# Cross-attention and ternary feed-forward on one core: ring piece 3 is loaded and summed behind the blocks of Wk

## The chip, the cores and the metric

The kernel runs on one core of a Trainium2 chip. The metric is the device time of one execution in microseconds, the median of several runs. The profile is one execution, taken by the hardware profiler; its span runs from the first to the last instruction.

## What is computed

```python
x   = layernorm(x)                                    # 16 x 256 x 512, fp32
q   = (ln(x) * g1 + b1) @ Wq + bq                     # 512 -> 512
k   = (ln(ctx) * g2 + b2) @ Wk + bk                   # 384 -> 512
v   = (ln(ctx) * g2 + b2) @ Wv + bv
x   = x_in + softmax(q @ k.T * 512**-0.5) @ v @ Wo + bo
h   = bitlinear(ln(x), w_fc) + gate * (ln(x) @ v.T @ fast_b.T @ u.T)   # 512 -> 2048
out = x_mid + bitlinear(relu(h) ** 2, w_proj)         # 2048 -> 512

def bitlinear(x, w):                                  # one scale for each row of w
    scale = max(mean(abs(w), axis=1), 1e-5)
    return x @ (clip(round(w / scale), -1, 1) * scale).T
```

The two weights of the feed-forward part are thus made ternary on the chip, which needs the sum of absolute values of each row first.

## The kernel before

The 4096 tokens are worked on in 8 groups of 512 tokens. For each group the attention part of the next group and the feed-forward part (16 `up` and 16 `down` blocks) of the current one are interleaved. Nearly all of the time goes there, and it is the same code before and after the change.

Ahead of the groups stands a setup, the prologue. It folds the attention weights, and makes the ternary weights. What matters here:

- `Wq` comes in four blocks, `Wk` in three, each of 256 KB. TensorE transposes them (`wqT:c`, `wkT:c`, L1185) into the banks H0 and H1 in turn; the product `bq` (L1190) lies between them. The results are read out by ScalarE or VectorE: `WqT` (L714, L902), the bq product into `x2a` (L910), `WkT` with the gains g2 multiplied in (L906).
- `M:c` (L1197) is the product of `WqT` and `WkT` for one block c of four. It is read twice: ScalarE makes its rounded half (L721), then VectorE, which waits for ScalarE, the rest (L913). `wvT:c` transposes Wv's blocks. A job n may use its bank only when job n-2 has been read: `wkT:1` waits for bq's evacuation, and `wvT:0` for `M:0` as read by VectorE.
- The feed-forward weights come in 32 pieces of 256 KB through a ring of 8 buffers (`ring:k`, L518), in groups of four. For each piece one engine sums absolute values: ScalarE (L846) most of them, VectorE (L1134) `abs:3`, `abs:7`, `abs:11` and a few more. When all four sums of a group are there, GpSimd makes the scales (`scale:j`, L670), VectorE their reciprocals (`invert:j`, L1122) and rounds the pieces (`round:k`, L1130). TensorE turns each (`turn:k`, L1378) and ScalarE stores its sign (`store:k`, L869). From piece 8 on a load waits until the buffer's piece has been rounded.
- `tb` makes the bias of the scores. GpSimd multiplies the three blocks of Wk by the evacuated bq product (L661, three instructions, each waiting for its Wk block); ScalarE sums each result (L836), one wait for each. Behind that ScalarE issues the load of Wo into the buffer that the products used (L840).
- Statistics: VectorE takes those of x (`xs01`, `xs23`, L1082 to L1091), GpSimd the power of them (`xs23`, L649, L650), ScalarE normalises (`nx0` and so on, L797), TensorE transposes the result (`n1T:t`, L1248).

The order of each engine is written out by hand in `PROLOGUE`. Each engine works its list strictly in order and waits on semaphores. The starts of the lists, of before:

```
pe    wqT:0 wqT:1 vecs wqT:2 wqT:3 bq:0 wkT:0 wkT:1 wkT:2 M:0 M:1 turn:0 turn:1 wvT:0 turn:2 turn:3 n1T:0 wvT:1 M:2
act   wqT:0 vecs wqT:2 abs:0 abs:1 wqT:3 g2 abs:2 tb Wo abs:4 abs:5 M:0 abs:6 M:1 nx0 wvT:0 store:0 store:1
dve   wqT:1 bqacc abs:3 bq:0 wkT:0 wkT:1 invert:0 wkT:2 xs01 xs23 abs:7 round:0 round:1 M:0 round:2 round:3
pool  scale:0 tb xs23 scale:1 scale:2 cs23
```

Of the kernel before, what the change touches and what calls it, by code (L numbers as in the profile page):

```python
# [199 lines left out]
def moved_by_act(b, kind):  # L200
# [3 lines left out]

PROLOGUE = {
# [4 lines left out]
    ).split(),  # L210
# [17 lines left out]
    ).split(),  # L228
    "dve": (
# [1214 lines left out]
```

## Time and profile before

| | |
|---|---|
| median of 3 runs | 780.21 us (779.91 to 780.46) |
| the profiled execution | 779.99 us, its span 778.2 us |
| TensorE busy | 766.5 us (98%) |
| VectorE busy | 547.6 us (70%) |
| ScalarE busy | 368.6 us (47%) |
| GpSimd busy | 107.4 us (14%) |

Times in the profile are microseconds from the start of the span. L12 is line 12 of the kernel. PE is TensorE, PEld its weight loads, DVE VectorE, ACT ScalarE, POOL GpSimd, SPq the sync engine's queue that issues DMAs. In a timeline a row begins with the start and the time that it covers; neighbouring instructions of the same kind are merged into one row (x8 is eight of them), and square brackets give the idle time before it and who ended it.

### The profile page before, as it was taken

How to read it: one execution, taken by the hardware profiler on the slowest of the kernel's cores; microseconds unless marked ns; L12 is line 12 of the kernel's file. 1: busy time of each engine (PE TensorE's matmuls, PEld its weight loads, DVE VectorE, ACT ScalarE, POOL GpSimd, SP SyncE). 2: the span in 40 equal slices, each digit the busy share in tenths (PEclk: the TensorE clock that was granted, in tenths of full speed). 3: DMA queues.
4: the chain of work that ended last, by engine and by line, in shares of the span. 5: the costliest groups of instructions: out<-in, count | busy, mean ns of one | idle time of the engine just before them, and what ended most of it. 6: DMA issues, size and time to landing. Idle time of an engine off the chain costs nothing.

```text
span 778.2 us, 10596 instructions
## 1 busy us (share of the span) xinstructions
PE 766.5 (98%) x3767; PEld 637.6 (82%) x3767; DVE 547.6 (70%) x1118; ACT 368.6 (47%) x690; POOL 107.4 (14%) x125
## 2 busy tenths in 40 slices
PE   7999999999999999999999999999999999999997
PEld 4678788888888888888888888888888888888886
DVE  5999766778676777667766786768667686656434
ACT  5998744354434535354434545254542644233332
POOL 3101300100211030110312020210202002100001
PEclk9999999999999999999999999999999999999999
DMA  8743431163115322063214422063212430040101
GB/s 315 248 150 109 63 88 41 21 96 87 56 40 84 58 72 85 13 97 69 81 42 65 65 75 96 1 99 70 90 41 41 75 88 1 1 54 9 47 0 55
DMA packets 180125, 56.20 MB, mean 72 GB/s; under 512 B 167620, under 2 KB 167894, under 8 KB 180072
## 3 DMA queue, kind: packets, MB, share of 16 engines
q1 hardware_dynamic: 149940, 50.79, 26.8%
q10 hardware_dynamic: 30132, 4.73, 3.8%
q8 instruction: 30, 0.49, 0.3%
q14 instruction: 23, 0.19, 0.1%
HBM read 26.92 MB, written 8.39 MB: 45 GB/s over the span
## 4 chain that ended last, share of the span: by engine, by line
PE 97%; DVE 1%; ACT 1%; issue 0%; DMA 0%; DVEq 0%; ACTq 0%
PE H L1357 30%; PE O L1338 29%; PE G L1220 26%; PE H L1363 4%; PE H L1220 1%; PE H L1197 1%; PE H L1204 1%; PE O L1412 1%; PE G L1304 1%; PE O L1378 1%; PE H L1185 1%; PE G L1248 0%; DMA Wq_s<-in_L_xattn_Wq_dram 0%; DVE x2a L1057 0%; PE O L1395 0%
## 5 line engine op out<-in xcount | busy, mean ns | idle before, releaser
L1338 PE MATMUL O<-projT,qbuf 128*128 128x512 f32 x992 | 242.1, 390 | 0.0
L1338 PEld LDWEIGHTS O<-projT,qbuf 128*128 128x128 f32 x992 | 185.0, 188 | 38.2
L779 ACT ACTIVATE rbuf<-H,scf 128x512 f32<-128x512 f32 x128 | 87.5, 684 | 124.9 <-DVE qbuf L1116 75.7
L1357 PE MATMUL H<-even_group,fcT 128*128 128x512 f32 x512 | 127.5, 391 | 0.0
L1357 PE MATMUL H<-odd_group,fcT 128*128 128x512 f32 x512 | 127.3, 391 | 0.0
L1112 DVE TENSOR_TENSOR rbuf<-rbuf 128x512 f32<-128x512 f32 x128 | 91.5, 723 | 45.9 <-ACT rbuf L779 45.9
L787 ACT ACTIVATE qbuf<-rbuf 128x512 fp32r<-128x512 f32 x125 | 78.5, 628 | 89.7 <-PE O L1338 62.7
L1116 DVE TENSOR_TENSOR qbuf<-rbuf,qbuf 128x512 fp32r<-128x512 f32 x125 | 85.9, 688 | 36.5 <-ACT qbuf L787 35.8
L1357 PEld LDWEIGHTS H<-odd_group,fcT 128*128 128x128 f32 x512 | 95.3, 188 | 19.3
L1357 PEld LDWEIGHTS H<-even_group,fcT 128*128 128x128 f32 x512 | 95.1, 188 | 19.2
L1220 PE MATMUL G<-Wvo,tT 128*128 128x512 f32 x270 | 64.7, 389 | 0.0
L1220 PEld LDWEIGHTS G<-Wvo,tT 128*128 128x128 f32 x270 | 50.6, 188 | 10.6
L1363 PE MATMUL H<-tstack,uT 128*128 128x512 f32 x128 | 49.8, 389 | 0.0
L654 POOL TENSOR_TENSOR nrs<-nrs,mhalf 128x1 f32<-128x1 f32 x32 | 25.5, 798 | 125.7 <-DVE nrs L954 125.7
L691 POOL TENSOR_TENSOR x2b<-xb,crow 128x512 f32<-128x512 f32 x16 | 24.3, 1550 | 120.2 <-DMA out_dram<-x2b 115.4
L741 ACT ACTIVATE pbuf<-G,nmax 128x256 f32<-128x256 f32 x29 | 13.7, 473 | 53.6 <-DVE nmax L941 53.6
L1220 PEld LDWEIGHTS G<-n2T,tT 128*128 128x128 f32 x261 | 34.1, 191 | 1.6
L1220 PE MATMUL G<-n2T,tT 128*128 128x256 f32 x261 | 34.8, 283 | 0.0
L760 ACT ACTIVATE tT<-G,tbias 128x512 fp32r<-128x512 f32 x23 | 15.8, 686 | 37.6 <-PE G L1220 37.6
L1220 PE MATMUL G<-odd_group,M 128*128 128x512 f32 x144 | 33.3, 389 | 0.0
L691 POOL TENSOR_TENSOR x2a<-xb,crow 128x512 f32<-128x512 f32 x12 | 17.5, 1489 | 112.6 <-DMA out_dram<-x2a 112.6
L1220 PEld LDWEIGHTS G<-odd_group,M 128*128 128x128 f32 x144 | 27.0, 188 | 5.6
(194 smaller groups left out, 989.0 us busy)
## 6 DMA issues: line engine op xcount, KB each, us to landing
xb<-in_x_dram SPq DMA_DIRECT2D x8, 1024.0 KB, 5.1
n_blocks<-n_rows SPq DMA_DIRECT2D x112, 64.0 KB, 2.3
ctxb<-in_ctx_dram SPq DMA_DIRECT2D x8, 768.0 KB, 4.3
n_blocks<-ctxb SPq DMA_DIRECT2D x112, 48.0 KB, 2.2
wring<-in_L_ffn_w_fc_dram SPq DMA_DIRECT2D x16, 256.0 KB, 6.2
wring<-in_L_ffn_w_proj_dram SPq DMA_DIRECT2D x16, 256.0 KB, 2.7
out_dram<-x2a SPq DMA_DIRECT2D x8, 512.0 KB, 2.7
x_blocks<-x_rows SPq DMA_DIRECT2D x56, 64.0 KB, 3.5
```

Source lines behind the costliest of these rows:

```text
L654: nc.gpsimd.tensor_tensor(nrs[:, t:t + 1], nrs[:, t:t + 1], mhalf[:, 0:1], ALU.pow).then_inc(rstd_made, 1)
L691: nc.gpsimd.tensor_tensor(x2[par][:, t, :], xb[:, t, :], crow[:, :], ALU.add).then_inc(res_made, 1)
L741: nc.scalar.activation(pbuf[:, t, :], bank[:, 0:S], ACT.Exp, bias=nmax[:, t:t + 1], scale=SM, accum_out=rowsum[:, t:t + 1]).then_inc(unit_ ...
L760: nc.scalar.activation(tT[:, HI, t, :], bank[:, :], ACT.Identity, bias=tbias[:, t:t + 1]).then_inc(unit_act, 1)
L779: nc.scalar.activation(rbuf[:, j % 2, :], banks[f"H{j % 2}"][:, :], ACT.Relu, scale=scf[:, j:j + 1]).then_inc(relu_made, 1)
L787: nc.scalar.activation(squares(b, j)[:, HI, :], rbuf[:, j % 2, :], ACT.Copy).then_inc(sqhi_made, 1)
L1112: nc.vector.tensor_tensor(rbuf[:, j % 2, :], rbuf[:, j % 2, :], rbuf[:, j % 2, :], ALU.mult).then_inc(square_made, 1)
L1116: nc.vector.tensor_tensor(squares(b, j)[:, LO, :], rbuf[:, j % 2, :], squares(b, j)[:, HI, :], ALU.subtract).then_inc(sqlo_made, 1)
L1220: mm = pe.matmul(bank, w, m, start=(first and i == 0), stop=(last and i == len(pairs) - 1))
L1338: mm = pe.matmul(banks[f"O{t}"][:, :], qbuf[:, j % 2, h, t * P:(t + 1) * P], projT[:, j, :], start=(j == 0 and h == HI), stop=(j == NFF - ...
L1357: pe.matmul(banks[f"H{j % 2}"][:, :], fcT[:, k, j * P:(j + 1) * P], xnT[:, h, k, :], start=(k == 0 and h == HI), stop=False)
L1363: pe.matmul(banks[f"H{j % 2}"][:, :], uT[:, j * P:(j + 1) * P], tstack[:, :], start=False, stop=True).then_inc(up_full, 1)
```

## The change

The order of loads on the SP queue was `Wk:2 ring:3 Wk:0 Wk:1 x:0`; it becomes `Wk:2 Wk:0 Wk:1 ring:3 x:0`. In VectorE's order the sum of ring piece 3 moves from before the evacuation of bq to behind those of Wk, and the reciprocal of the first group's scales from between the evacuations of Wk to behind the statistics of x. The lists of TensorE, ScalarE and GpSimd are the same.

```diff
@@ -204,7 +204,7 @@
 PROLOGUE = {
     "sp": (
-        "Wq:0 Wq:1 ring:0 Wq:2 bqrow ring:1 bo Wq:3 ring:2 Wk:2 ring:3 Wk:0 Wk:1 x:0 ring:4 ring:5 ring:6 "
+        "Wq:0 Wq:1 ring:0 Wq:2 bqrow ring:1 bo Wq:3 ring:2 Wk:2 Wk:0 Wk:1 ring:3 x:0 ring:4 ring:5 ring:6 "
@@ -227,7 +227,7 @@
     "dve": (
-        "wqT:1 bqacc abs:3 bq:0 wkT:0 wkT:1 invert:0 wkT:2 xs01 xs23 abs:7 round:0 round:1 M:0 round:2 round:3 "
+        "wqT:1 bqacc bq:0 wkT:0 wkT:1 wkT:2 abs:3 xs01 xs23 invert:0 abs:7 round:0 round:1 M:0 round:2 round:3 "
```

## Rows read from the trace of the kernel before

**Rows 1.** The page's first part: busy time, share of the span, instructions.

```profile
PE 766.5 (98%) x3767; PEld 637.6 (82%) x3767; DVE 547.6 (70%) x1118; ACT 368.6 (47%) x690; POOL 107.4 (14%) x125
```

**Rows 2.** Stretches: length; PE, PEld, DVE, ACT, POOL busy; granted clock; DMA.

```profile
20.00:23.00 3.00, 2.87 (x27) 2.42 (x25) 3.00 (x8) 3.00 (x6) 0.34 (x1) 1.00 0.96 341
23.00:40.00 17.00, 16.88 (x88) 9.67 (x86) 15.97 (x37) 16.57 (x38) 1.70 (x4) 1.00 0.73 225
40.00:60.00 20.00, 19.38 (x124) 15.53 (x125) 18.64 (x42) 18.11 (x45) 2.14 (x9) 1.00 0.48 154
60.00:100.00 40.00, 38.48 (x240) 32.75 (x241) 35.12 (x86) 30.45 (x63) 12.19 (x15) 1.00 0.35 78
```

**Rows 3.** The chain that ended last, 9 to 24 us: start, length, what.

```profile
13.48 0.17 DVE inverse_scales L1122
...
14.37 5.40 PE H L1197 x16
19.77 0.45 PE O L1378 x8
```

**Rows 4.** Timeline of TensorE, 3 to 22 us.

```profile
3.72 1.94 PE L1185 MATMUL H<-ident,Wq_s 128*128 128x128 f32 x8 [3.72 <-DMA Wq_s<-in_L_xattn_Wq_dram]
...
11.23 0.60 PE L1185 MATMUL H<-ident,Wk_s 128*128 128x128 f32 x4
...
20.05 0.61 PE L1185 MATMUL H<-ident,Wv_s 128*128 128x128 f32 x4
...
21.23 0.63 PE L1248 MATMUL G<-ident,nrm 128*128 128x128 f32 x4
```

**Rows 5.** Timeline of VectorE, 10 to 31 us.

```profile
10.26 0.69 DVE L1134 TENSOR_REDUCE asum<-wring 128x1 f32<-128x512 f32 x1 [0.85 <-DMA wring<-in_L_ffn_w_fc_dram]
11.43 0.69 DVE L910 COPY x2a<-H 128x512 f32<-128x512 f32 x1 [0.48 <-PE H L1190]
...
13.56 0.66 DVE L906 TENSOR_TENSOR WkT<-H,g2row 128x512 f32<-128x512 f32 x1
14.20 2.47 DVE L1082 BATCH_NORM_STATS2 xst<-xb 128x6 f32<-128x512 f32 x4
...
17.87 0.88 DVE L1130 TENSOR_SCALAR rounded<-wring,inverse_scales 128x512 f16<-128x512 f32 x2
19.23 0.62 DVE L913 SCALAR_TENSOR_TENSOR M<-H,vcols,M 128x384 fp32r<-128x384 f32 x1 [0.49 <-ACT M L721]
...
30.25 1.35 DVE L1134 TENSOR_REDUCE asum<-wring 128x1 f32<-128x512 f32 x2
```

**Rows 6.** Timeline of ScalarE, 15 to 21 us.

```profile
15.97 0.72 ACT L836 ACTIVATE x2a<-x2a,vcols 128x512 f32<-128x512 f32 x1 [0.42 <-POOL x2a L661]
...
18.57 0.56 ACT L721 ACTIVATE M<-H,vcols 128x384 fp32r<-128x384 f32 x1
...
19.80 0.58 ACT L721 ACTIVATE M<-H,vcols 128x384 fp32r<-128x384 f32 x1
```

**Rows 7.** Timeline of GpSimd, 11 to 33 us.

```profile
11.88 0.24 POOL L670 TENSOR_SCALAR scf<-asum 128x4 f32<-128x4 f32 x1 [9.07 <-ACT sprow L846]
12.21 3.73 POOL L661 TENSOR_TENSOR x2a<-Wk_s,x2a 128x512 f32<-128x512 f32 x3
17.45 1.34 POOL L649 TENSOR_TENSOR xrs<-xrs,mhalf 128x4 f32<-128x4 f32 x1 [1.51 <-DVE xrs L1091]
...
19.83 0.51 POOL L670 TENSOR_SCALAR scf<-asum 128x4 f32<-128x4 f32 x1 [0.77 <-ACT sprow L846]
31.08 0.23 POOL L670 TENSOR_SCALAR scf<-asum 128x4 f32<-128x4 f32 x1 [10.74 <-DVE asum L1134]
31.39 1.04 POOL L649 TENSOR_TENSOR crs<-crs,mhalf 128x4 f32<-128x4 f32 x1
```

**Rows 8.** Timeline of the SP queue: ring 3, then the two Wk blocks.

```profile
5.04 0.43 SPq L518 DMA_DIRECT2D wring<-in_L_ffn_w_fc_dram  x1
5.52 0.91 SPq L554 DMA_DIRECT2D Wk_s<-in_L_xattn_Wk_dram  x2
```

## The prediction

> **What bounds the kernel now.** The page's first part comes first: TensorE is busy 766.5 of 778.2 us [rows 1], so only what delays TensorE, or takes work from it, can move the time. The change lies wholly in the setup, so the stretches come next. TensorE is busy 2.87 of the 3 us from 20 to 23, 16.88 of 17 from 23 to 40, 19.38 of 20 up to 60 and 38.48 of 40 up to 100 [rows 2]. All its idle time from 20 to 100 us is 0.13 + 0.12 + 0.62 + 1.52 = 2.4 us: a delay put in at 20 us has nearly nothing behind it to vanish into. ScalarE is as full there (3.00 of 3.00, 16.57 of 17) and VectorE nearly so.
>
> Then the chain of waits through the touched place [rows 3, 5]: VectorE empties the bank of the bq product (11.43), the Wk evacuations follow with a 0.17 us reciprocal (`invert:0`) before the last of them (13.48), and TensorE computes M:0 and M:1 from 14.37 to 19.77. What it may do next is `turn:0 turn:1 wvT:0`; wvT:0 reuses M:0's bank and waits until VectorE has read it.
>
> The chain does not show what stands just beside it, so the engines' own orders are read. wvT:0 starts at 20.05 [rows 4]. VectorE's M:0 (19.23, 0.62 us, to 19.85) waited 0.49 us for ScalarE's M:0 [rows 5]. ScalarE did that at 18.57, directly behind `tb` (its third piece starts at 15.97), the issue of Wo, abs:4 and abs:5 [rows 6]. ScalarE's `tb` waits for GpSimd's three products, 12.21 to 15.94, and GpSimd runs them behind `scale:0`, at 11.88 [rows 7]. So a second chain, GpSimd's products, ScalarE's tb, M:0, reaches wvT:0 with a slack of about 0.1 us.
>
> **Part by part.** *The loads.* Ring 3 is issued at 5.04 [rows 8], between Wk:2 and Wk:0. Behind the change Wk:0 and Wk:1 go one place (0.48 us, the step from 5.04 to the next issue at 5.52) earlier and ring 3 two places (0.95) later. The SP queue issues the same number, and no wait stands between them; x:0 behind them keeps its place. Worth of the earlier Wk: nothing. wkT:0 starts at 11.23 directly behind the bq product [rows 4], and wkT:1 needs the bank that VectorE empties from 11.43 [rows 5]. Bounds: 0 to -0.2 us; I take 0. Ring 3 lands at about 10.26 now (VectorE starts its sum then, having waited on that transfer) [rows 5]; 1 us later is far ahead of its new use at 14.1.
>
> *VectorE.* abs:3 (0.69 us) leaves the place before bq:0. It ended at 10.95 and VectorE then idled 0.48 us for TensorE before 11.43 [rows 5], so its removal frees nothing. `invert:0` leaves the place before wkT:2: that evacuation starts at 13.48 in place of 13.56 [rows 3, 5], and M:0 and M:1 each 0.08 us sooner. This is the whole gain on TensorE, and it is worth something only if wvT:0 doesn't wait for the second chain. Behind wkT:2 abs:3 now runs from about 14.12 to 14.81. xs01, xs23, abs:7, round:0 and round:1 slide by 0.69 - 0.08, a little less for overlap: the statistics start at 14.73 in place of 14.20, round:0 at 18.48 in place of 17.87 [rows 5]. turn:0 could start at 19.69 and finds its piece at 18.96: hidden. VectorE still reaches its M:0 at about 19.35.
>
> *The wait that moves, which decides.* `scale:0` on GpSimd needs all four sums of group 0, abs:3 among them; GpSimd's order `scale:0 tb xs23` is not changed. So `tb` now stands behind a sum that VectorE does 3.86 us later. Step by step: abs:3 ends at 14.81. From such a sum to GpSimd's start is 0.15 us: the pair at 30.25 takes 1.35, its first half ends at 30.93 and scale:2 starts at 31.08 [rows 5, 7]. scale:0 runs 14.96 to 15.20 (0.24); the next GpSimd work starts 0.08 behind (31.08 + 0.23 to 31.39), hence 15.28. Before it was 12.21: later by 3.07 us. Products until 19.01 (3.73), ScalarE's third tb piece at 15.97 + 3.07 = 19.04, Wo's issue and abs:4, abs:5 behind, ScalarE's M:0 at 21.64, VectorE's at 22.30 to 22.92, wvT:0 at 23.06. TensorE, done with turn:1 at about 20.1, stands still for almost 3 us.
>
> Queued behind ScalarE's wait are the Wo load, abs:4 to abs:6, M:1 and nx0; behind VectorE's M:0 the rounds 2 onwards, and so the SP queue's ring loads 10 onwards and the loads behind them. The xs23 power on GpSimd (17.45 now) starts at 19.1 and ends by 20.6, ahead of nx0: hidden by the larger delay.
>
> *What is given back.* M:1 on ScalarE starts at 19.80, just after TensorE finished it at 19.77, though ScalarE's step before it allowed 19.65 [rows 3, 6]. With TensorE early, these 0.15 us come back: nx0 is late by 3.07 - 0.15 = 2.92, and n1T:0, which started at 21.23 for nx0's sake [rows 4], by the same. From there on TensorE, ScalarE and VectorE stand at the same points of their orders as before, and all DMAs gated by rounding move along. I find no wait on a load that is independent of them. Sum: +2.9 us.
>
> *Unknown sizes.* The third product (17.75 to 19.01) now lies beside round:0. Where GpSimd's work lies beside a round now, the power of 17.45 takes 1.34 against 1.04 us for that of 31.39, and scale:1 at 19.83 takes 0.51 against 0.23 [rows 7]. So the products may take 0 to 0.45 us more (the end is one round's 0.44, half the pair at 17.87 [rows 5]); I take 0, because the product starts first, and keep 0.45 for the range. The latency of 0.15 may be 0.05 to 0.2. Own range of the forecast: +2.6 to +3.5.
>
> The Trainium skill ("SBUF — State Buffer", "Who interferes with whom") says that VectorE in its two-port modes and GpSimd hold a shared port for a whole instruction, and the first to start makes the other wait. The two longer rows agree in direction. By it round:0 would wait for the third product, not the reverse, which leaves the sum as it is.
>
> **Rivals.** *(A) The clock falls too.* TensorE would have a hole of 2.9 us and then until 25 us only short transposes with waits between. The granted clock reads 1.00 in every stretch, but eight transposes take 1.94 us at the start (0.24 each) and four take 0.60 at 11.23 (0.15) [rows 2, 4]: the level of half speed (1.2 GHz) shows at the start, after TensorE had stood still, the full one (2.4 GHz) after it had worked. If it returns, 1.5 to 3.2 us of the work from 22 us on are paid twice: the upper end is half of the 6.3 us from 3.72 until the fast level was reached about 10, the lower half of that. Time 779.99 + 2.9 + 1.5 to 3.2 = 784.4 to 786.1. Against it: 40 us with 1.52 us of holes show no fall; no hole in this trace is near 3 us. Chance 0.13.
>
> The Trainium skill ("TensorE: Matmul & The Clock Gate", "HAM oscillation — how this bites in real kernels") states that idle gaps between bursts throttle the engine again. No row here has such a gap; by that rule the time is rival A's.
>
> *(B) The hole is closed again: not slower.* Place: the waits from 23 to 100 us. TensorE idles 2.26 us there [rows 2]; if these waits were bound to something that does not move (loads in flight), they would absorb that much of the 2.9 and leave 0.6 or so: 780.6. It decides from 1.4 us absorbed. Against it: those waits name VectorE and ScalarE, which stand behind the same late step, and the loads are gated by rounds. Chance 0.09, the half-absorbed cases among it.
>
> *(C) The second chain doesn't bite: the change does what it looks like.* M:0 0.08 us earlier and Wk up to 0.2: 779.7 to 779.9. It needs GpSimd's tb to start before abs:3; the code forbids it. Chance 0.03.
>
> **How the numbers follow.** Profiled execution of before: 779.99 (span 778.2 and 1.8 around it), 0.2 below the median 780.21. 779.99 + 2.9 = 782.9, on the median 783.1; I say 783.1, chance 0.75. Its own range is 782.6 to 783.9. The range reaches down to 782.0 for a part absorbed, and up to 785.2 into rival A: 782.0 to 785.2. A measurement can tell about 0.2%, 1.6 us, from no change. Slower: forecast, rival A and part of B, 0.90; within: 0.07; faster: 0.03 (what B and C leave for an effect not seen).
>
> **What would show it.** After the change: abs:3 at about 14.1, scale:0 near 15.0, products from 15.3, ScalarE's M:0 at 21.6, wvT:0 at 23.1, n1T:0 at 24.2, and the same distance of about 2.9 us in the steady part. The prediction is wrong if GpSimd's products start near 12.2, if TensorE has no hole after 20.1, if four transposes behind the hole take near 1 us (rival A), or if the offset shrinks between 25 and 100 us (rival B).

## The result and the profile after

The changed kernel takes 786.02 us (median of 5 runs, 785.73 to 789.66) against 780.21 us (779.85 to 780.46): 5.8 us more. The ratio over all runs is 1.0083 with a 95% interval of 1.0061 to 1.0106; it lies above the 1.0074 of the two medians because it takes in the run of 789.66. Forecast were 783.1 us, 2.9 us more, and a range up to 785.2. The sign and the first step were right; the size was half of what came.

TensorE's timeline of the changed kernel, 14 to 36 us; it answers to [rows 4]:

```profile
14.86 5.40 PE L1197 MATMUL H<-WkT,WqT 128*128 128x384 f32 x16 [0.89 <-DVE WkT L906]
20.09 0.61 PE L1378 MATMUL O<-identh,rounded 128*128 128x128 f16 x8
23.52 1.11 PE L1185 MATMUL H<-ident,Wv_s 128*128 128x128 f32 x4 [2.82 <-DVE M L913]
24.42 1.06 PE L1378 MATMUL O<-identh,rounded 128*128 128x128 f16 x8
25.28 1.06 PE L1248 MATMUL G<-ident,nrm 128*128 128x128 f32 x4
26.13 0.89 PE L1185 MATMUL H<-ident,Wv_s 128*128 128x128 f32 x4
26.86 2.75 PE L1197 MATMUL H<-WkT,WqT 128*128 128x384 f32 x8
...
30.55 0.60 PE L1248 MATMUL G<-ident,nrm 128*128 128x128 f32 x4
32.27 3.70 PE L1204 MATMUL H<-x2a,WvT 128*128 128x512 f32 x8 [1.11 <-DVE M L913]
```

Beside the same points of before (M:0 14.37, wvT:0 20.05, M:2 22.13, n1T:1 25.82, wvo:0 26.27) the lag grows in four steps: 0.49 us at M:0, 3.47 at wvT:0, 4.73 at M:2 and n1T:1, 6.00 at wvo:0. Behind that it stays: the span is 784.2 against 778.2, again 6.0. There are two holes, not one. The first (2.82 us) is the predicted one. Behind it four transposes (wvT:0, n1T:0) take 1.11 and 1.06 us instead of 0.61 and 0.63: the clock fell. The second (1.11 us, before wvo:0) no step of the prediction has.

GpSimd, 15 to 24 us, for [rows 7]: scale:0 now waits for VectorE's sum, and the products behind it take 3.73 us as before.

```profile
15.50 0.24 POOL L670 TENSOR_SCALAR scf<-asum 128x4 f32<-128x4 f32 x1 [12.69 <-DVE asum L1134]
15.82 3.73 POOL L661 TENSOR_TENSOR x2a<-Wk_s,x2a 128x512 f32<-128x512 f32 x3
```

VectorE, 14 to 33 us, for [rows 5]:

```profile
14.63 0.68 DVE L1134 TENSOR_REDUCE asum<-wring 128x1 f32<-128x512 f32 x1
...
18.99 1.24 DVE L1130 TENSOR_SCALAR rounded<-wring,inverse_scales 128x512 f16<-128x512 f32 x2
22.84 0.62 DVE L913 SCALAR_TENSOR_TENSOR M<-H,vcols,M 128x384 fp32r<-128x384 f32 x1 [2.61 <-ACT M L721]
...
28.57 0.75 DVE L1068 SCALAR_TENSOR_TENSOR bvrep<-x2a,vcols,borow 128x512 f32<-128x512 f32 x1 [2.54 <-DMA x2a<-in_L_xattn_Wo_dram]
29.36 2.33 DVE L1072 SCALAR_TENSOR_TENSOR bvrep<-x2a,vcols,bvrep 128x512 f32<-128x512 f32 x3
31.60 0.61 DVE L913 SCALAR_TENSOR_TENSOR M<-H,vcols,M 128x384 fp32r<-128x384 f32 x1
```

The row at 28.57 is `coacc`, which sums bv @ Wo. It stands ahead of M:2 in VectorE's order, and it waited 2.54 us for the load of Wo. Then M:2, and with it the bank that wvo:0 needs, comes behind the 3.1 us of coacc. The chain of waits (start, length, what) goes the same way and passes by TensorE's first hole and slow clock altogether:

```profile
15.82 3.74 POOL x2a L661 x3
19.56 0.02 issue
19.59 0.82 ACT x2a L836 x2
20.41 0.02 issue
20.43 8.12 DMA x2a<-in_L_xattn_Wo_dram
28.55 0.02 issue
28.57 0.76 DVE bvrep L1068
```

The same places in the kernel before: ScalarE's issue of Wo, its landing, VectorE's coacc and M:2, TensorE's wvo:0.

```profile
16.82 0.41 ACTq L840 DMA_DIRECT2D x2a<-in_L_xattn_Wo_dram  x1
DMA to landing us min/median/max: 5.1/5.1/5.1
22.33 0.75 DVE L1068 SCALAR_TENSOR_TENSOR bvrep<-x2a,vcols,borow 128x512 f32<-128x512 f32 x1
25.59 0.62 DVE L913 SCALAR_TENSOR_TENSOR M<-H,vcols,M 128x384 fp32r<-128x384 f32 x1 [0.16 <-PE H L1185]
26.27 3.70 PE L1204 MATMUL H<-x2a,WvT 128*128 128x512 f32 x8
```

Wo's issue is 3.61 us later than before (20.43 for 16.82), like the products. But its landing takes 8.1 us for 5.1, and the 0.4 us by which it used to be early are used up: 3.61 + 3.0 - 0.4 = 6.2 us, and coacc starts 6.24 us later (28.57 for 22.33). M:2 had 0.2 us to spare before (its wait of 0.16 us for TensorE), so it is 6.0 us later, and wvo:0 with it.

The granted clock of TensorE in the changed kernel, in stretches of 1 us (columns as in [rows 2]). TensorE does nothing from 21 to 23; the clock falls in the stretch from 23, still before wvT:0 starts (cut finer it reads 0.99 up to 23.3 and 0.50 from there), and stays at the level of half speed (1.2 GHz) until near 26.7.

```profile
22.00:23.00 1.00, 0.00 (x0) 0.00 (x0) 0.15 (x1) 1.00 (x4) 0.00 (x0) 1.00 0.85 285
23.00:24.00 1.00, 0.48 (x3) 0.48 (x4) 1.00 (x3) 1.00 (x4) 0.51 (x1) 0.65 0.98 321
25.00:26.00 1.00, 1.00 (x9) 1.00 (x8) 1.00 (x3) 1.00 (x3) 0.00 (x0) 0.50 1.00 364
26.00:27.00 1.00, 1.00 (x7) 1.00 (x6) 0.03 (x1) 0.94 (x2) 0.00 (x0) 0.64 1.01 391
27.00:28.00 1.00, 1.00 (x5) 0.60 (x4) 0.00 (x0) 0.94 (x2) 0.00 (x0) 1.00 1.02 399
```

So there were three candidates to part: the products behind scale:0 (the prediction's step), the clock's fall (rival A), and Wo's landing (nobody's).

### The profile page after: what moved, and what is told of

It reads as the page before. It is cut to its first block, busy times and chain, and to the rows that moved or that the text cites. A ratio compares the mean times of both kernels' runs of the same rounds, so it can differ in the third digit from the quotient of the medians.

```text
span 784.2 us, 10596 instructions
## 1 busy us (share of the span) xinstructions
PE 769.0 (98%) x3767; PEld 639.7 (82%) x3767; DVE 548.7 (70%) x1118; ACT 368.9 (47%) x690; POOL 107.4 (14%) x125
## 3 DMA queue, kind: packets, MB, share of 16 engines
q1 hardware_dynamic: 149940, 50.79, 26.7%
q10 hardware_dynamic: 30132, 4.73, 3.8%
## 4 chain that ended last, share of the span: by engine, by line
PE 95%; DMA 2%; DVE 1%; POOL 1%; ACT 1%; issue 0%; SPq 0%; POOLq 0%; DVEq 0%; ACTq 0%
PE H L1357 30%; PE O L1338 29%; PE G L1220 26%; PE H L1363 4%; PE H L1220 1%; PE H L1204 1%; DMA x2a<-in_L_xattn_Wo_dram 1%; PE O L1412 1%; PE G L1304 1%; DMA Wq_s<-in_L_xattn_Wq_dram 1%; POOL x2a L661 0%; PE H L1185 0%; PE H L1197 0%; PE O L1378 0%; PE G L1248 0%
```

## The experiments

Each was timed together with the kernel before, whose medians there were 780.2 to 780.5 us. The ratio goes by all runs (4 to 10 of each kernel), so it can differ a little from that of the medians. Each kernel has one trace; where a reading below rests on a trace, it is that of one execution.

| kernel | median us | ratio to before, 95% interval |
|---|---|---|
| tb_first | 780.46 | 0.9998 (0.9989 to 1.0007) |
| dve_only | 787.31 | 1.0093 (1.0070 to 1.0116) |
| sp_only | 781.14 | 1.0019 (1.0007 to 1.0031) |
| wo_late | 791.79 | 1.0145 (1.0130 to 1.0160) |
| warm | 786.71 | 1.0087 (1.0071 to 1.0102) |
| wo_early | 784.24 | 1.0047 (1.0032 to 1.0062) |
| wo_early_warm | 785.72 | 1.0070 (1.0055 to 1.0085) |
| ctx_late | 784.78 | 1.0053 (1.0036 to 1.0070) |
| warm12 | 789.92 | 1.0124 (1.0109 to 1.0139) |
| wo_early_warm12 | 782.68 | 1.0030 (1.0019 to 1.0042) |
| wo_alone | 787.50 | 1.0091 (1.0076 to 1.0106) |
| warm_both | 786.71 | 1.0079 (1.0062 to 1.0096) |

**Is GpSimd's order the root?** On top of the change:

```diff
     "pool": (
-        "scale:0 tb xs23 scale:1 scale:2 cs23 ...
+        "tb scale:0 xs23 scale:1 scale:2 cs23 ...
```

> The changed kernel with one more edit: GpSimd makes the three tb products before scale:0, so that they no longer stand behind VectorE's late sum of piece 3. Theory (the whole loss comes from the products standing behind scale:0): products start near 12.3 us as before the change, TensorE has no hole behind turn:1, Wo is issued near 16.9 and lands before VectorE wants it, time 780.0 to 780.7. Rival (the moved loads or VectorE's own order cost by themselves): 782 or more remains.

The whole loss is gone: 780.46 us. GpSimd's rows, 9 to 20 us:

```profile
12.65 3.74 POOL L661 TENSOR_TENSOR x2a<-Wk_s,x2a 128x512 f32<-128x512 f32 x3 [9.84 <-DVE x2a L910]
16.47 0.25 POOL L670 TENSOR_SCALAR scf<-asum 128x4 f32<-128x4 f32 x1
```

The products wait for bq's evacuation again, Wo lands 5.2 us after its issue, and TensorE has no hole. So everything that follows is set off by the one wait. The change with this edit is not measurably faster than the kernel before either: there is no version here that beats it.

**Which half of the change?** VectorE's new order with the old loads (edit to the changed kernel):

```diff
-... Wk:2 Wk:0 Wk:1 ring:3 x:0
+... Wk:2 ring:3 Wk:0 Wk:1 x:0
```

> The kernel before with VectorE's new order alone; the loads keep their old order. Theory (the sum behind Wk's evacuations is the cause): 785.4 to 786.2, as the full change. Rival (the reordered loads have a share: TensorE's M:0 began 0.49 us later in the changed kernel): 0.5 to 0.7 us less than the full change, times the Wo load's sharing, so 784.5 to 785.5.

787.31 us (785.76 to 790.06), 1.1 us above the upper end of what was expected. Its interval, 1.0070 to 1.0116, holds the change's 1.0083: VectorE's order is the whole cause within what can be told. In its profiled execution (787.72) 1.7 us more are the clock's: there it fell not behind the first hole but behind the second, and wvo:0 took 5.40 us instead of 3.70.

The new loads with the old order (edit to the kernel before):

```diff
-... Wk:2 ring:3 Wk:0 Wk:1 x:0
+... Wk:2 Wk:0 Wk:1 ring:3 x:0
```

> The kernel before with the new order of loads alone. Theory: ring 3 lands later than 10.3, so that abs:3, still ahead of bq:0 on VectorE, may start as late as 11.3 and hold bq's evacuation by up to 0.6 us; 780.2 to 780.9. Rival (the 0.49 us by which M:0 was late in the changed kernel is due to the loads): M:0 starts near 14.9 and the time is 780.7 or more.

781.14 us, above the expected range by 0.2 and slower than before by 0.7. VectorE's row, 8 to 20 us, shows the hold that was expected:

```profile
11.60 0.69 DVE L1134 TENSOR_REDUCE asum<-wring 128x1 f32<-128x512 f32 x1 [1.88 <-DMA wring<-in_L_ffn_w_fc_dram]
12.20 0.68 DVE L910 COPY x2a<-H 128x512 f32<-128x512 f32 x1
```

The sum still stands ahead of bq's evacuation and ends at 12.29, after the bq product (11.92). That holds the evacuation by 0.3 us. Its ten runs fall into two groups, six from 780.05 to 781.27 and four from 782.94 to 783.85; 0.7 is the difference of the medians. M:0 starts at 15.36 and the time is above 780.7, so what the rival named is there as well. Whether the loads alone made the 0.49 us by which M:0 was late in the changed kernel is still not shown: with the new loads M:0 starts anywhere from 14.05 (wo_alone) to 15.36, with the old at 14.37 before, 14.54 in dve_only and 14.66 in wo_late, one trace each. It goes with the time at which TensorE reaches its fast level: the median transpose of Wk takes 380 ns in the changed kernel and 273 before. Such a late start need not belong to the kernel: in the trace of tb_first M:0 starts at 15.23, in an execution of 780.85 us, and its median is still that of the kernel before.

**Can a late Wo do it alone?** In the kernel before:

```diff
-... abs:2 tb Wo abs:4 abs:5 M:0 abs:6 M:1 nx0 ...
+... abs:2 tb abs:4 abs:5 M:0 abs:6 M:1 Wo nx0 ...
```

> The kernel before with one edit: ScalarE issues the load of Wo behind M:1 (near 20.4 us) instead of behind tb (16.8). No other work is late, TensorE gets no hole at 20 us and its clock should stay at 1.00. Theory (Wo's late landing alone sets the final loss of the change): Wo lands at 25.5 to 28.5, VectorE's coacc waits, M:2's and wvo:0's steps follow, and the time is 783.5 to 786.5. Rival (the hole and the fall of the clock set the loss, the Wo wait is hidden in them): 780.2 to 781.0.

791.79 us, 11.4 more, and far beyond both. VectorE's rows, 17 to 45 us, and TensorE's:

```profile
32.33 0.75 DVE L1068 SCALAR_TENSOR_TENSOR bvrep<-x2a,vcols,borow 128x512 f32<-128x512 f32 x1 [9.74 <-DMA x2a<-in_L_xattn_Wo_dram]
```

```profile
20.35 0.61 PE L1185 MATMUL H<-ident,Wv_s 128*128 128x128 f32 x4
...
36.02 5.68 PE L1204 MATMUL H<-x2a,WvT 128*128 128x512 f32 x8 [9.29 <-DVE M L913]
```

Nothing but Wo is late (wvT:0 at 20.35, no hole at 20), and Wo, issued at 20.1, lands after 12.2 us. Here the rounds were not late, so rings 10 to 14 were issued from 19.92 to 22.9, in the first 3 us of Wo's flight, where the changed kernel issues them from 23.89 on. Behind a hole of 9.3 us the clock is at half speed and wvo:0 takes 5.68 instead of 3.70 us. The wait and the slower wvo:0, 9.7 + 2.0 = 11.7, are the growth of the span (789.9). The expectation's landing of 5.1 to 8.1 us was too short: it too took a landing from another place.

**Is the clock's fall paid?** Filling matmuls into a bank that is overwritten later, in the changed kernel's first hole (they add work that the result doesn't use):

```diff
-... M:0 M:1 turn:0 turn:1 wvT:0 ...
+... M:0 M:1 turn:0 turn:1 warm wvT:0 ...
+                    elif kind == "warm":
+                        for _ in range(24):
+                            pe.matmul(banks["O3"][:, 0:P], ones[:, :], ident[:, :], start=True, stop=True)
```

> The changed kernel with 24 more matmuls of 128x128 (ones by identity, into the bank that turn:3 overwrites) between turn:1 and wvT:0, so that TensorE works through the hole at 20 to 23 us. Theory (the late landing of Wo near 28.6 us sets the loss, the fall of the clock before it is hidden by that wait): the granted clock stays 1.00 from 20 to 27 us, M:2 starts about 1.3 us sooner than 26.9, yet VectorE still waits for Wo and the time stays at 785.5 to 786.3. Rival (the clock's fall is paid in full): 784.4 to 784.9.

The filling was mis-sized: 5.58 us, so wvT:0 started at 25.83, 2.3 us later than in the changed kernel. The clock stayed at 1.00, M:2 started at 27.59, and the time came out at 786.71, only 0.7 more and 0.4 above the expected range. VectorE again waited for Wo (3.4 us; it landed after 9.0). TensorE could be 2.3 us later at wvT:0 and the end hardly moved: it is the chain through Wo that counts. With 12 calls, which fit the hole (`range(12)`):

> The changed kernel with 12 filling matmul calls in place of 24 (24 took 5.58 us, 2 to 3 us more than the hole; 12 should take 2.8). Theory (Wo's landing sets the loss): granted clock 1.00 up to 27 us, M:2 near 25.3 instead of 26.9, VectorE still waits for Wo until 28 to 29, wvo:0 near 32.3, time 785.4 to 786.4. Rival (the clock's fall at 23 us is paid in the end): 784.3 to 784.9.

```profile
20.01 2.90 PE L1383 MATMUL O<-ident,ones 128*128 128x128 f32 x24
22.99 0.66 PE L1185 MATMUL H<-ident,Wv_s 128*128 128x128 f32 x4
...
25.04 2.75 PE L1197 MATMUL H<-WkT,WqT 128*128 128x384 f32 x8
...
32.57 6.70 PE L1204 MATMUL H<-x2a,WvT 128*128 128x512 f32 x8 [3.23 <-DVE M L913]
```

(TensorE's timeline.) M:2 is early as expected, and still wvo:0 starts at 32.57. But the time is 789.92, which neither theory had. Arriving sooner at the same wait made the second hole longer, 3.23 us, and the clock fell there: wvo:0 took 6.70 instead of 3.70 us, 3.0 of the 3.9 us above the changed kernel (in the two profiled executions 3.0 of 3.3; the other 0.3 is the later start of wvo:0). In the changed kernel the slow stretch lay under short transposes, and Wo's landing covered it. To test this, 12 more calls ahead of turn:6 (`warm2`; they wait until piece 2 is stored and write into bank O2):

```diff
-... turn:5 turn:6 n1T:1 wvo:0 ...
+... turn:5 warm2 turn:6 n1T:1 wvo:0 ...
```

> The changed kernel with 12 filling matmul calls in the first hole, as before, and 12 more ahead of turn:6, so that TensorE also works through most of its wait for Wo. Theory: with the first hole filled alone, the second (3.2 us) let the clock fall under wvo:0, whose eight matmuls took 6.70 instead of 3.70 us, and that is why it came out at 789.9; with both filled the clock stays at 1.00, VectorE still waits for Wo until 28.5 to 29, wvo:0 starts near 32.5 and takes 3.7, time 785.7 to 786.7, which is Wo's landing alone. Rival (the filling itself costs, by the read port or by power): 788 or more.

```profile
28.81 2.90 PE L1386 MATMUL O<-ident,ones 128*128 128x128 f32 x24
...
33.11 3.70 PE L1204 MATMUL H<-x2a,WvT 128*128 128x512 f32 x8 [0.74 <-DVE M L913]
```

786.71 us, at the upper end of the expected range. The clock stays at 1.00 in all of 20 to 40 us, wvo:0 takes 3.70 again, and Wo's late landing (9.2 us here) alone makes the loss: coacc and wvo:0 both start 0.84 us later than in the changed kernel (29.41 and 33.11), and the profiled execution is 0.82 us longer.

**What is left without Wo?** The tb products go to other buffers, so that Wo can be loaded ahead of tb (issued at 11.40), with the other orders as changed:

```diff
-... abs:2 tb Wo abs:4 ...
+... abs:2 Wo tb abs:4 ...
-                        act.wait_ge(tb_made, KC)
+                        act.wait_ge(job_full, JOBS.index(("bq", 0)) + 1)
-   ... x2a[:, m, :] (products), x2a[:, KC, :] (bq's evacuation)
+   ... tbuf[m], nrm[:, 1, :]          # tbuf = [ybuf[0], ybuf[1], nrm[:, 0, :]]
```

> The changed kernel with the tb products and the evacuated bq product in other buffers, so that ScalarE issues Wo's load ahead of tb (near 12 us) into its free place. GpSimd's products stay late and so does M:0. Theory (hole of 2.9 to 3.6 us at 20 us, plus the clock, plus Wo's landing as the last and longest): coacc finds Wo there, TensorE's second hole before wvo:0 goes, and what is left is the hole and the slow clock: 783.4 to 785.0. Rival (Wo's landing isn't the bound): 785.8 or more.

784.24 us: within the range. The second hole is gone. The first ends at 22.56, and the clock then falls. One of the four runs, 782.48 us, has a mean clock of 0.999 where the others (783.94 to 785.10) have 0.997, which speaks for a fall that doesn't come in every execution. The edit takes away a little more than Wo's wait. ScalarE no longer issues the load between tb and abs:4, and from its third tb piece to abs:4 it now takes 0.72 us (19.28 to 20.00) instead of 1.35 (19.59 to 20.94). So M:0 gains 0.6 us here that the changed kernel doesn't have, and the hole is 1.51 us, not 2.82. With the filling too, first with 24 calls:

> Both edits: Wo's load ahead of tb, and 24 matmuls through the hole. Theory: only the late tb products are left, which was the prediction's own sum: 783.0 to 783.9. The difference to the kernel with Wo early alone is the price of the clock's fall, 0.3 to 1.5 us. Rival (more of the loss is elsewhere): 784.5 or more.

Here the mis-sized filling is paid: 785.72, 1.8 us above the expected range, with wvT:0 at 25.82. That 5.58 us of filling cost nearly nothing in `warm` and 1.5 us here is the difference between being hidden behind Wo and not. With 12 calls:

> Wo's load ahead of tb and 12 filling matmul calls. With Wo early alone TensorE's hole ended at 22.56 (2.5 us late) and its clock then fell. Theory: what is left is the hole's 2.5 to 3.1 us, so 782.8 to 783.8, and 0.5 to 1.5 us less than Wo early alone (784.24). Rival (the clock costs nothing measurable): no less than 784.0.

```profile
20.98 2.90 PE L1384 MATMUL O<-ident,ones 128*128 128x128 f32 x24
23.71 0.60 PE L1186 MATMUL H<-ident,Wv_s 128*128 128x128 f32 x4
```

782.68 us (782.38 to 783.37), 0.1 below the range. This is +2.5 us. With the 0.6 us that ScalarE gains it makes about 3.1 by this estimate, near the 2.9 of the prediction's own sum. Against wo_early the clock's fall is worth 1.4 to 1.6 us there (3.9 against 2.5 us above the kernel before, or by the two medians).

**Why does Wo take 8 us?** ctx's load (768 KB), issued just after ring 8 and 9 and at about Wo's time, moved behind ring 11:

```diff
-... ring:8 ring:9 ctx:0 ring:10 ring:11 ring:12 ...
+... ring:8 ring:9 ring:10 ring:11 ctx:0 ring:12 ...
```

> The changed kernel with the load of ctx (768 KB) moved behind ring 11 on the SP queue, so that less is in flight beside Wo. Theory (Wo takes 8.1 us instead of 5.1 because ring 8, ring 9 and ctx, released by the late rounds, go out just ahead of it and share the engines): Wo lands after 5.3 to 6.8 us, near 26 to 27 us, and the time falls to 784.2 to 785.2. Rival (Wo shares with whatever is there, ring 10 to 13 take ctx's place): landing stays near 8 us and the time at 786.

784.78 us is in the expected range, but Wo's landing fell only to 7.7 us (issue 20.13), where 5.3 to 6.8 were expected: what the rival says of rings 10 and 11 taking ctx's place is half right. Its four runs span 783.93 to 787.07. In the slowest, the profiled one, wvo:0 takes 5.40 us behind a hole of 1.99: the second-hole clock fall again. Then ctx and all behind it held back until Wo is in:

```diff
                 elif kind == "ctx":
+                    sp.wait_ge(wo_in, 16)
```

> The changed kernel where the SP queue waits for Wo to have landed before it issues ctx and all loads behind it; only ring 8 and 9 are then beside Wo. Theory (Wo takes 8 us because it shares the engines with all that is in flight, whatever it is): Wo lands 4.5 to 6 us after its issue, near 25.5, VectorE's coacc hardly waits, and the time is 783.8 to 785.3 (the hole and the clock are left). Rival (Wo's landing is slow for another reason): 8 us, 786 or more.

Wo lands 6.9 us after its issue (19.62 to 26.55), longer than expected, and the time is 787.50, worse: neither the theory's nor the rival's. wvo:0 starts at 30.27, two us sooner than in the changed kernel. But a ring load issued at 30.64, behind those held back, lands only at 37.49 (6.85 us), and VectorE's sum, round and bvrep behind it are late: a hole of 1.90 us comes before wvo:2 (40.18), and the clock falls behind it, so that seven of its matmuls take 4.97 us instead of 3.17.

So Wo's landing goes with what else is under way. From the rate at which the DMA engines moved data while Wo was in flight, less the 1.05 MB of Wo itself, comes an estimate of what went beside it (in part the columns must go together, since a longer flight sees more loads):

| kernel | landing us | GB/s meanwhile | beside Wo, MB |
|---|---|---|---|
| before | 5.1 | 317 | 0.6 |
| wo_alone | 6.9 | 227 | 0.5 |
| ctx_late | 7.7 | 292 | 1.2 |
| the change | 8.1 | 329 | 1.6 |
| dve_only | 8.5 | 324 | 1.7 |
| warm_both | 9.2 | 322 | 1.9 |
| wo_early | 9.8 | 373 | 2.6 |
| wo_late | 12.2 | 296 | 2.6 |

In sp_only and tb_first it was 5.1 and 5.2 us, as before. One kernel falls out: in wo_alone no more went beside Wo than before, and in the last two microseconds of its flight the engines moved only 127 and 25 GB/s. What held that last part is not settled.

## Why the prediction was half right

- *Bound, and where a delay stays.* Right: the lag is 6.00 us at wvo:0 and 6.0 at the end of the span, nothing is given back. Rival B is out, and C with it. The 0.15 us expected back at M:1 came back (ScalarE's M:0 is 3.61 us later, its M:1 3.46).
- *The loads.* Costed at nothing. In the full change no cost could be told apart from the spread (dve_only is no faster than it). Alone they cost 0.7 us, of which the hold of bq's evacuation by abs:3 makes 0.3 in its trace; the rest is not explained.
- *VectorE's sums.* Right, though 0.5 us late: abs:3 at 14.63 for about 14.1, the pair of rounds hidden. The gain of 0.08 us was worth nothing.
- *The wait that moves.* Right in mechanism and size: scale:0 at 15.50, products at 15.82, a shift of 3.61 us for the 3.07 expected, the 0.5 between being TensorE's later start. The hole ended at 23.52 (23.06 expected). tb_first shows it as the root.
- *The port.* The products took 3.73 us as taken; the rounds beside them gave way: the pair at 18.99 took 1.24 instead of 0.88 us. By the Trainium skill's rule ("SBUF — State Buffer", "Who interferes with whom") the first to start holds the port, and the trace agrees.
- *"I find no wait on a load that is independent of them."* This is the step that failed. Wo's load was named as queued behind ScalarE's wait, and then moved along by the same 3 us, with its 5.1 us of landing taken as fixed. It was not: the later issue falls together with ring 8, ring 9 and ctx (19.86 to 21.1), where before it had gone 1.6 us ahead of them (16.82 and 18.38). Its landing grew by 3.0 us. The term stood at nothing. With it the chain through Wo comes to 3.6 + 3.0 - 0.4 - 0.2 = 6.0 us, the whole measured growth of the span; without it this chain would have been only 3.0 us late, hidden behind TensorE's own 4.7 (hole and clock), and the time about 784.9 by this estimate, inside the range. wo_early and wo_early_warm12 take the wait away and come out at 784.24 and 782.68, wo_late makes one without the rest and costs 11.4 us. That the landing grew because of the loads beside it is what the table of landings supports, but no experiment takes away those loads alone and gets 5.1 us back.
- *The clock.* Rival A came true in its observation (transposes at about half speed, 1.1 us for four) and its range, 784.4 to 786.1, even holds the time; but for another reason. In the changed kernel the fall is hidden behind Wo: the kernel with the clock kept up and Wo still late (warm_both, 786.71) is no faster; its Wo took 9.2 us to land, and the whole difference of 0.8 us to the changed kernel's profiled execution is Wo's. The fall is paid where Wo is early (1.4 to 1.6 us) and where it falls under wvo:0 (3 us in warm12). By the Trainium skill's rule ("TensorE: Matmul & The Clock Gate", "HAM oscillation — how this bites in real kernels") idle gaps bring the slow level back; the gaps of its example are longer than the holes here, and the trace agrees with the direction, though not alike each time: at the end of 2.82 us it fell in the changed kernel, behind 2.81 us in dve_only the same transposes took 0.66 us, and it fell only at the second hole, where wvo:0 took 5.40. Whether one of the changed kernel's five runs, 789.66, is such a case is open: its mean clock is 0.994 where three others have 0.998, but the fifth has 0.995 and took 785.88, and neither of these two has a trace.
- *The range.* The forecast's own upper end of 783.9 doesn't follow from its numbers; 780.21 + 3.5 gives 783.7. The measured time is above both, and above the 785.2 that was to reach into rival A.

## What to carry to other kernels

A wait that moves should be followed through every engine's order, DMA issues included, and a load that moves needs a new landing time: what it took at the old place (5.1 us here) says little of what it takes among other loads (6.9 to 12.2). Before an operation is moved behind others on one engine, look at what a third engine has queued behind the operation that needs its result; here one pair of words exchanged in GpSimd's list (`tb scale:0`) took away all 5.8 us. Where two lags lead to the same wait, making the earlier one shorter can cost: in warm12 TensorE then stood longer at the second, and the clock fell under bigger matmuls.

## What the runs showed that was not expected

- One load of 1 MB took from 5.1 to 12.2 us to land, mostly by what else was under way.
- TensorE's clock fell behind holes of 1.5 to 3.2 us in some kernels and not in others, and what it costs depends on the work that follows: eight matmuls of 128x512 in fp32 took 3.70 us at the full level and 5.40 to 6.70 when the fall reached them.
- 24 calls of a 128x128 fp32 matmul show as 48 instructions and take 5.58 us, twice what the transposes of the same size would (four in 0.44 us from start to start).
